# A new layout of the first two tiles' work, and nine products of the identity on PE

## The chip, the cores and the metric

The kernel runs on one core of a Trainium2 chip. The metric is device time in microseconds of one execution, taken several times; the median counts. A profile of one execution gives the trace from which the rows below come.

## What is computed

A gated cross attention and a gated feed-forward layer, in f32, on x and a context, both of 16 batches x 64 channels x 512 positions:

```
xn  = layernorm(x)                      # over the 512 positions
q   = Wq @ instance_norm(xn) + bq       # 64 x 512, for each batch
k   = Wk @ instance_norm(ctx) + bk
s   = Ws @ ctx + bs
a   = softmax(q^T k)                    # 512 x 512, for each batch
mean = a s ;  std = sqrt(relu(a s^2 - mean^2))
x   = x + tanh(g1) * (instance_norm(ctx) * std + mean)
x   = x + tanh(g2) * (layernorm(x) @ W^T)   # W from 4-bit weights, scales and zeros
```

## The kernel before, in words

Two batches are one tile of 128 partitions, so there are 8 tiles. The scores of a tile are made in 8 chunks of 128 query positions (4 for each batch b), numbered g = 0 to 63 over all tiles; chunk g belongs to tile t = g // 8. Every engine has its program written out in order, and semaphores connect them.

The query weights and key weights are multiplied first (multiply_weights, L266), so that scores are x^T (Wq^T Wk) ctx plus bias terms. To keep f32 accuracy at the speed of the rounded type fp32r, operands are split into a high part (a cast) and a low part (the rest). project(t) (L279) makes q of tile t in side_bank by three products. q is split by keep_q_hi on ACT (L434) and keep_q_lo on DVE (L609). The operands of the scores are then stacked on 128 partitions: q_both (q hi over q lo), c_both (the context's hi twice), q_with_x (q hi over x hi), c_with_bias (the context's lo over the bias rows). For b = 0 of tile 0 ACT and DVE write these stacks; for all others SP issues seven copies by DMA (stack, L211). It waits for c_lo_done before the first four and for q_lo_done before the last three. scores(g) (L287) waits for the stacks of its batch where j is 0, and does two products of 512 columns (L296, L297).

Then, chunk by chunk: DVE takes the maximum (L616), ACT the exponentials (L442), DVE the reciprocal of their sum (L623), POOL the normalised probabilities (normalise_probs, L831), PE turns them (turn, L306, four transposes), ACT copies them back (L450) and PE weighs the values with them (weigh, L322). The values come from value_product(t) (L333), kept by DVE (keep_values) and squared by POOL (square_values, L836). Scores run three chunks ahead (AHEAD_S), exponentials two (AHEAD_E), weighing two behind.

During tile t the engines also prepare tile t + 2: statistics on DVE (L559, L565), the power -0.5 on POOL (L812), xn and the context normalised on DVE (L586, L599), their hi parts cast on DVE (L594, L604), their lo parts on POOL (x_lo in split_x_lo, L818; c_lo in split_c_lo, L824), and project(t + 2) on PE at chunk 7. The weights of the feed-forward are prepared in tiles 1 to 7, and the feed-forward itself follows the last tile.

The start: SP loads x, params and the context of tile 0, then tile 1. DVE makes the statistics of x, then of the context (L539 to L550); xn, x_hi, x_lo and w_a_lo come before the context's parts. PE starts with L271 when params are there.

## Time and profile before

| | us |
|---|---|
| median of 3 runs | 186.06 |
| lowest and highest | 185.04, 186.35 |
| the profiled execution, its time | 186.42 |
| its span in the trace | 184.6 |
| PE busy in the span | 167.2 |
| DVE, ACT, POOL busy | 141.0, 118.0, 120.4 |

The span runs from the first to the last instruction of the trace; the time of the same execution is 1.8 us longer. A transfer's row stands on SPq, the queue that issues it, with the time of the issue alone; what waits for its landing names it as releaser. A column of idle time gives what ended the wait.

### The profile page before, as it was taken

The page shows a single profiled execution, that of the slowest core. Times are in us where ns is not written, and L with a number is a line of the kernel's source. Part 1 is how long each engine was busy: PE and PEld are TensorE (multiplying, and loading weights), DVE is VectorE, ACT ScalarE, POOL GpSimd, SP SyncE. Part 2 cuts the span into 40 slices and gives each one's busy share as a digit, 9 for nine tenths or more (in the row PEclk, how much of TensorE's full clock was granted, in tenths as well). Part 3 has the DMA queues.
Part 4 walks back from the last instruction along what each step waited for, and adds up shares of the span by engine and source line. Part 5 has one row for each costly group of instructions (what it writes and reads, how often), then busy time and mean ns, then how long its engine had stood idle before and what let it go on. Part 6 is the DMA issues. An engine that isn't in the chain of part 4 may idle for free.

```text
span 184.6 us, 3489 instructions
## 1 busy us (share of the span) xinstructions
PE 167.2 (91%) x1128; PEld 147.1 (80%) x1128; DVE 141.0 (76%) x311; ACT 118.0 (64%) x261; POOL 120.4 (65%) x145
## 2 busy tenths in 40 slices
PE   1554999999999999999999999999999979789992
PEld 0432889999999999999999999998789867567881
DVE  2897696689859887986988798676159679988851
ACT  2253575978598678859867885995569995232110
POOL 1455586917955896799589679944328959966310
PEclk9999999999999999999999999999999999999999
DMA  6408566883796699679679966356100000111212
GB/s 169 166 21 202 186 159 138 237 201 86 184 319 153 155 287 245 162 216 286 139 170 249 283 145 153 78 134 151 44 0 0 4 0 0 57 62 60 111 57 114
DMA packets 14321, 25.75 MB, mean 139 GB/s; under 512 B 2336, under 2 KB 2464, under 8 KB 14304
## 3 DMA queue, kind: packets, MB, share of 16 engines
q1 hardware_dynamic: 14304, 25.54, 52.2%
q8 instruction: 9, 0.15, 0.4%
q14 instruction: 8, 0.07, 0.1%
HBM read 9.67 MB, written 2.10 MB: 64 GB/s over the span
## 4 chain that ended last, share of the span: by engine, by line
PE 76%; DVE 9%; ACT 4%; issue 4%; POOL 3%; DMA 2%; SPq 0%; ACTq 0%; POOLq 0%
PE pv_bank L322 28%; PE turn_bank L306 14%; PE score_bank L296 8%; PE score_bank L297 8%; PE side_bank L333 3%; PE score_bank L377 3%; PE score_bank L371 3%; PE score_bank L370 3%; DVE X L667 2%; DMA CTX<-in_context 2%; PE side_bank L342 2%; ACT probs L442 1%; PE side_bank L283 1%; DVE result L692 1%; DVE stats L673 1%
## 5 line engine op out<-in xcount | busy, mean ns | idle before, releaser
L831 POOL TENSOR_SCALAR probs<-probs,rden 128x512 f32<-128x512 f32 x64 | 50.9, 796 | 32.2 <-DVE rden L623 32.0
L322 PE MATMUL pv_bank<-probs_t,values 128*128 128x128 f32 x512 | 67.7, 276 | 0.0
L442 ACT ACTIVATE probs<-score_bank,neg_max 128x512 f32<-128x512 f32 x64 | 44.1, 690 | 31.4 <-DVE neg_max L616 30.8
L322 PEld LDWEIGHTS pv_bank<-probs_t,values 128*128 128x128 f32 x512 | 62.4, 192 | 2.1 <-issue 1.7
L616 DVE TENSOR_REDUCE neg_max<-score_bank 128x1 f32<-128x512 f32 x64 | 43.5, 682 | 15.0 <-PE score_bank L297 14.4
L306 PE MATMUL turn_bank<-ident,probs 128*128 128x128 f32 x256 | 38.8, 275 | 1.1 <-ACT probs_t L450 1.0
L450 ACT COPY probs_t<-turn_bank 128x512 f32<-128x512 f32 x64 | 37.1, 581 | 3.2 <-PE turn_bank L306 3.0
L306 PEld LDWEIGHTS turn_bank<-ident,probs 128*128 128x128 f32 x256 | 31.1, 142 | 5.7 <-POOL probs L831 1.1
L296 PE MATMUL score_bank<-c_both,q_both 128*128 128x512 f32 x64 | 29.3, 458 | 2.3 <-ACT q_with_x L494 2.3
L297 PE MATMUL score_bank<-c_with_bias,q_with_x 128*128 128x512 f32 x64 | 26.4, 412 | 0.0
L296 PEld LDWEIGHTS score_bank<-c_both,q_both 128*128 128x128 f32 x64 | 13.0, 202 | 4.6 <-issue 2.9
L623 DVE RECIPROCAL rden<-den 128x1 f32<-128x1 f32 x64 | 9.9, 154 | 6.1 <-ACT probs L442 6.0
L297 PEld LDWEIGHTS score_bank<-c_with_bias,q_with_x 128*128 128x128 f32 x64 | 13.0, 203 | 1.7
L370 PE MATMUL score_bank<-w_hi,xt_hi 128*128 128x512 f32 x32 | 12.8, 402 | 0.0
L371 PE MATMUL score_bank<-w_lo,xt_hi 128*128 128x512 f32 x32 | 12.7, 397 | 0.0
L442 ACT ACTIVATION_READ_ACCUMULATOR probs<-score_bank,neg_max 128x1 f32 x64 | 12.6, 197 | 0.0
L634 DVE TENSOR_TENSOR VAR<-pv_bank,mean_sq 64x512 f32<-64x512 f32 x16 | 11.1, 694 | 0.5
L865 POOL TENSOR_TENSOR rstd<-var_eps,power 128x1 f32<-128x1 f32 x8 | 6.7, 834 | 7.0 <-DVE var_eps L679 7.0
L824 POOL TENSOR_TENSOR c_lo<-CTX,c_hi 128x512 fp32r<-128x512 f32 x8 | 10.7, 1337 | 0.8 <-DVE c_hi L604 0.8
L818 POOL TENSOR_TENSOR x_lo<-xn,x_hi 128x512 fp32r<-128x512 f32 x7 | 9.0, 1282 | 3.1 <-DVE x_hi L594 3.1
L860 POOL TENSOR_TENSOR CTX<-CTX,VAR 128x512 f32<-128x512 f32 x7 | 9.4, 1348 | 2.1 <-ACT VAR L465 2.1
L609 DVE SCALAR_TENSOR_TENSOR q_lo<-side_bank,b_a,q_hi 128x512 fp32r<-128x512 f32 x8 | 6.0, 749 | 5.6 <-ACT q_hi L434 5.6
(99 smaller groups left out, 243.6 us busy)
## 6 DMA issues: line engine op xcount, KB each, us to landing
c_both<-c_hi SPq DMA_DIRECT2D x30, 128.0 KB, 2.6
X<-in_x SPq DMA_DIRECT2D x8, 256.0 KB, 3.0
CTX<-in_context SPq DMA_DIRECT2D x8, 256.0 KB, 4.1
ctx_now<-in_context SPq DMA_DIRECT2D x8, 256.0 KB, 2.9
sz<-in_scales_zeros SPq DMA_DIRECT2D x4, 512.0 KB, 6.7
out<-result SPq DMA_DIRECT2D x8, 256.0 KB, 2.0
q_with_x<-x_hi SPq DMA_DIRECT2D x15, 128.0 KB, 2.3
c_with_bias<-c_lo SPq DMA_DIRECT2D x15, 128.0 KB, 2.9
```

Source lines behind the costliest of these rows:

```text
L296: pe.matmul(score_bank[g % SBANKS][:, :], q_both[b][:, rows], c_both[b][:, :], start=True, stop=False)
L297: pe.matmul(score_bank[g % SBANKS][:, :], q_with_x[b][:, rows], c_with_bias[b][:, :], start=False, stop=True).then_inc(scores_done, 1)
L306: last = pe.transpose(turn_bank[g % 2][:, P * i:P * i + P], probs[g % PROBS][:, P * i:P * i + P], ident[:, :])
L322: last = pe.matmul(pv_bank[b][:, P * j:P * j + P], values[t % 2][:, i, b, :, :].rearrange("p a c -> p (a c)"), probs_t[g % PROBS_T][:, P * ...
L370: pe.matmul(ffn_bank[u % 2][:, :], hi, w_hi[:, g, :], start=(g == 0), stop=False)
L371: pe.matmul(ffn_bank[u % 2][:, :], hi, w_lo[:, g, :], start=False, stop=False)
L442: act.activation(probs[g % PROBS][:, :], score_bank[g % SBANKS][:, :], ACT.Exp, bias=neg_max[:, c:c + 1], accum_out=den[:, c:c + 1]).then_ ...
L450: act.copy(probs_t[g % PROBS_T][:, :], turn_bank[g % 2][:, :]).then_inc(turned_kept, 1)
L616: dve.tensor_reduce(neg_max[:, c:c + 1], score_bank[g % SBANKS][:, :], AX_X, ALU.max, negate=True).then_inc(max_done, 1)
L634: dve.tensor_tensor(VAR[rows_of(b), t, :], pv_bank[b][C:P, :], mean_sq[b][C:P, :], ALU.subtract).then_inc(var_done, 1)
L824: pool.tensor_tensor(c_lo[t % 2][:, :], CTX[:, t, :], c_hi[t % 2][:, :].bitcast(F32), ALU.subtract).then_inc(c_lo_done, 1)
L831: pool.tensor_scalar(probs[g % PROBS][:, :], probs[g % PROBS][:, :], rden[:, c:c + 1], 1.0, ALU.mult, ALU.mult).then_inc(probs_done, 1)
```

## The change

It touches only the work of tiles 0, 1 and part of tile 2.

- SP loads the context of tile 0 first, then x; params go over ACT's queue. The copies of tile 0, b = 1 become four (first_stacked) in place of seven.
- PE multiplies ident by itself: spin(6) ahead of the weights' transposes, spin(1) behind them, spin(2) ahead of the first product. They write score_bank[0], which scores(0) writes anew.
- q of tile 0 is made by plain f32 products of w_a with xn (project_first), in pieces of 128 (FIRST, into turn_bank[1]) and 384 columns (REST, into side_bank). w_a_hi and w_a_lo are made later, on POOL, for project(1).
- The stacks of tile 0 are written directly from the banks, in these pieces, by ACT (hi) and DVE (lo: first_lo). The pieces of c and x for b = 1 are split between ACT, POOL and the copies.
- PE does scores 0 to 3 first, then turn(0), value_product(0); project(1) comes after turn(2), project(2) moves from chunk 7 to chunk 8.
- On DVE the maxima and reciprocals of chunks 0 to 2 stand between the statistics of tile 1 and the pieces of q. The casts x_hi and c_hi of tiles 1 and 2 move from DVE to ACT (cast_x_hi, cast_c_hi).
- On POOL, normalise_probs(0) and (1) surround the power of tile 1; after normalise_probs(2) come split_x_lo(1), square_values(0) and the memset of averages, then normalise_probs(3); split_c_lo(1) comes at chunk 2. For tile 2, the power stands behind normalise_probs(7), and split_x_lo(2) at chunk 7.

The rest of the diff renumbers semaphores. Its core:

```diff
+            sp.dma_start(CTX[:, 0, :], context_tiles[0]).then_inc(first_loaded[0][1], DMA)
             sp.dma_start(X[:, 0, :], x_tiles[0]).then_inc(first_loaded[0][0], DMA)
-            sp.dma_start(params_sb[:, :], params).then_inc(params_loaded, DMA)
-            sp.dma_start(CTX[:, 0, :], context_tiles[0]).then_inc(first_loaded[0][1], DMA)
             load(1, *first_loaded[1])
             load_ctx_now(0)
+            sp.wait_ge(first_c_both, 3)
+            sp.dma_start(c_both[1][0:C, :].bitcast(F32), c_both[1][C:P, :].bitcast(F32)).then_inc(first_stacked, DMA)
+            sp.wait_ge(first_q_hi, 4)
+            sp.dma_start(q_both[1][0:C, :].bitcast(F32), q_hi[0][C:P, :].bitcast(F32)).then_inc(first_stacked, DMA)
+            sp.dma_start(q_with_x[1][0:C, :].bitcast(F32), q_hi[0][C:P, :].bitcast(F32)).then_inc(first_stacked, DMA)
             sp.wait_ge(c_lo_done, 1)
-            stack(0, 1, *x_and_context_copies)
-            sp.wait_ge(q_lo_done, 1)
-            stack(0, 1, *q_copies)
+            sp.dma_start(c_with_bias[1][0:C, :].bitcast(F32), c_lo[0][C:P, :].bitcast(F32)).then_inc(first_stacked, DMA)
             load_ctx_now(1)
...
@@ -263,6 +293,10 @@
 
         @block.tensor
         def _(pe):
+            def spin(n):
+                for _ in range(n):
+                    pe.matmul(score_bank[0][:, FIRST], ident[:, :], ident[:, :], start=True, stop=True)
+
             def multiply_weights():
 
                 w_q, w_k = w_turned[:, 0:P], w_turned[:, P:2 * P]
@@ -270,16 +304,27 @@
                 pe.wait_ge(ident_ready, 1)
                 pe.transpose(turn_bank[0][:, 0:P], w_qk[:, 0:P], ident[:, :])
                 pe.transpose(turn_bank[0][:, P:2 * P], w_qk[:, P:2 * P], ident[:, :]).then_inc(w_turned_done, 1)
+                spin(1)
                 pe.wait_ge(w_turned_kept, 1)
-                pe.matmul(pv_bank[1][:, 0:P], w_q, w_k, start=True, stop=True)
-                pe.matmul(pv_bank[1][:, P:P + 1], w_k, b_qk[:, 0:1], start=True, stop=True)
-                pe.matmul(pv_bank[1][:, P + 1:P + 2], w_q, b_qk[:, 1:2], start=True,
-                          stop=True).then_inc(w_multiplied, 1)
+                pe.matmul(pv_bank[0][:, 0:1], w_k, b_qk[:, 0:1], start=True, stop=True)
+                pe.matmul(pv_bank[0][:, 1:2], w_q, b_qk[:, 1:2], start=True,
+                          stop=True).then_inc(biases_multiplied, 1)
+                pe.matmul(pv_bank[1][:, 0:P], w_q, w_k, start=True, stop=True).then_inc(w_multiplied, 1)
+
+            def project_first():
+
+                pe.wait_ge(xn_done, 1)
+                pe.wait_ge(w_a_ready, 1)
+                pe.matmul(turn_bank[1][:, FIRST], w_a[:, :], xn[:, FIRST], start=True, stop=True).then_inc(first_q_done, 1)
...
-                    pe.wait_ge(stacked[b], STACK * (t + 1))
+                if t > 0:
+                    if j == 0:
+                        pe.wait_ge(stacked[b], STACK * t)
+                elif g == 0:
+                    pe.wait_ge(first_c_both, 2)
+                    pe.wait_ge(first_c_lo, 1)
+                    pe.wait_ge(bias_rows_ready, 1)
+                    pe.wait_ge(first_x_rows, 1)
+                    pe.wait_ge(first_q_copied, 1)
+                    pe.wait_ge(first_q_lo, 1)
+                elif g == 1:
+                    pe.wait_ge(first_q_copied, 2)
+                    pe.wait_ge(first_q_lo, 2)
+                elif g == JC:
+                    pe.wait_ge(first_stacked, 4 * DMA)
+                    pe.wait_ge(first_q_lo, 4)
+                    pe.wait_ge(bias_rows_ready, 2)
...
 
+            pe.wait_ge(ident_ready, 1)
+            spin(6)
             multiply_weights()
-            pe.wait_ge(w_split, 1)
-            project(0)
-            pe.wait_ge(bias_rows_ready, 2)
-            for g in range(AHEAD_S):
+            spin(2)
+            project_first()
+            for g in range(AHEAD_S + 1):
                 scores(g)
-            pe.wait_ge(q_lo_done, 1)
-            project(1)
-            scores(AHEAD_S)
-            value_product(0)
-            pe.wait_ge(ident_ready, 1)
 
             for t in range(TILES):
                 for c in range(CHUNKS):
@@ -396,10 +453,17 @@
                     if c % 2 == 1 and g + AHEAD_S < LAST:
                         scores(g + AHEAD_S)
                         scores(g + AHEAD_S + 1)
-                    if c == 7 and t + 2 < TILES:
+                    if c == 7 and 1 <= t and t + 2 < TILES:
                         pe.wait_ge(s_kept, t + 2)
                         project(t + 2)
+                    if g == CHUNKS:
+                        pe.wait_ge(s_kept, 2)
+                        project(2)
                     turn(g)
+                    if g == 0:
+                        value_product(0)
+                    if g == 2:
+                        project(1)
                     if c == 3 and t + 1 < TILES:
...
@@ -477,21 +554,31 @@
                 act.copy(xt_hi[u % 2][:, :], xt_bank[u % 2][:, :]).then_inc(xt_hi_done, 1)
 
 
+            act.dma_start(params_sb[:, :], params).then_inc(params_loaded, DMA)
             act.wait_ge(w_turned_done, 1)
             act.copy(w_turned[:, :], turn_bank[0][:, 0:2 * P]).then_inc(w_turned_kept, 1)
-            act.wait_ge(params_loaded, DMA)
+            act.wait_ge(ctxn_done, 1)
+            act.copy(c_both[0][0:C, :], CTX[0:C, 0, :]).then_inc(first_c_both, 1)
+            act.wait_ge(w_multiplied, 1)
+            act.copy(w_a[:, :], pv_bank[1][:, 0:P]).then_inc(w_a_ready, 1)
+            act.copy(c_both[0][C:P, :], CTX[0:C, 0, :]).then_inc(first_c_both, 1)
+            act.wait_ge(b_ready, 1)
+            act.wait_ge(first_q_done, 1)
+            act.activation(q_both[0][0:C, FIRST], turn_bank[1][0:C, FIRST], ACT.Identity,
+                           bias=b_a[0:C, 0:1]).then_inc(first_q_hi, 1)
+            act.wait_ge(first_q_hi, 1)
+            act.copy(q_with_x[0][0:C, FIRST], q_both[0][0:C, FIRST].bitcast(F32)).then_inc(first_q_copied, 1)
+            act.copy(c_both[1][C:P, :], CTX[C:P, 0, :]).then_inc(first_c_both, 1)
+            act.wait_ge(first_q_done, 2)
+            act.activation(q_both[0][0:C, REST], side_bank[0:C, REST], ACT.Identity,
+                           bias=b_a[0:C, 0:1]).then_inc(first_q_hi, 1)
+            act.wait_ge(first_q_hi, 2)
+            act.copy(q_with_x[0][0:C, REST], q_both[0][0:C, REST].bitcast(F32)).then_inc(first_q_copied, 1)
+            act.activation(q_hi[0][C:P, FIRST], turn_bank[1][C:P, FIRST], ACT.Identity,
+                           bias=b_a[C:P, 0:1]).then_inc(first_q_hi, 1)
+            act.activation(q_hi[0][C:P, REST], side_bank[C:P, REST], ACT.Identity,
+                           bias=b_a[C:P, 0:1]).then_inc(first_q_hi, 1)
             act.activation(tanh_g[:, :], gates, ACT.Tanh).then_inc(gates_ready, 1)
-            act.wait_ge(w_multiplied, 1)
-            act.copy(w_a_hi[:, :], pv_bank[1][:, 0:P]).then_inc(w_hi_ready, 1)
-            act.wait_ge(ctxn_done, 1)
-            act.copy(c_both[0][0:C, :], CTX[0:C, 0, :]).then_inc(stacked[0], DMA)
-            act.copy(c_both[0][C:P, :], CTX[0:C, 0, :]).then_inc(stacked[0], DMA)
-            act.wait_ge(b_ready, 1)
-            act.wait_ge(q_done, 1)
-            keep_q_hi(0)
-            act.wait_ge(q_hi_done, 1)
-            act.copy(q_both[0][0:C, :], q_hi[0][0:C, :].bitcast(F32)).then_inc(stacked[0], DMA)
-            act.copy(q_with_x[0][0:C, :], q_hi[0][0:C, :].bitcast(F32)).then_inc(stacked[0], DMA)
             for g in range(AHEAD_E):
                 exponentials(g)
...
-                    if c == 0 and t + 1 < TILES:
+                    if g == 0:
+                        cast_x_hi(1)
+                    if g == 1:
+                        cast_c_hi(1)
+                    if g == 6:
+                        cast_x_hi(2)
+                    if g == 7:
+                        cast_c_hi(2)
+                    if g == 2:
+                        keep_q_hi(1)
+                    if c == 0 and 1 <= t and t + 1 < TILES:
                         keep_q_hi(t + 1)
...
                                          X[:, u, :], ALU.mult, ALU.add).then_inc(result_done, 1)
 
 
-            first_statistics()
+            def first_lo(n, b, bank, columns, hi):
+
+                dve.wait_ge(first_q_hi, n)
+                dve.scalar_tensor_tensor(q_both[b][C:P, columns], bank[rows_of(b), columns], b_a[rows_of(b), 0:1],
+                                         hi[rows_of(b), columns].bitcast(F32), ALU.add,
+                                         ALU.subtract).then_inc(first_q_lo, 1)
+
+            first_statistics(1, CTX, first_loaded[0][1], 1.0, EPS)
+            first_statistics(0, X, first_loaded[0][0], 1.0 + EPS, EPS * EPS)
+            normalise_ctx(0)
             normalise_x(0)
-            keep_x_hi(0)
-            dve.wait_ge(x_hi_done, 1)
-            dve.tensor_tensor(x_lo[:, :], xn[:, :], x_hi[0][:, :].bitcast(F32), ALU.subtract).then_inc(x_lo_done, 1)
-            dve.wait_ge(w_hi_ready, 1)
-            dve.tensor_tensor(w_a_lo[:, :], pv_bank[1][:, 0:P], w_a_hi[:, :].bitcast(F32),
-                              ALU.subtract).then_inc(w_split, 1)
-            dve.tensor_copy(b_a[:, :], pv_bank[1][:, P:P + 2]).then_inc(b_ready, 1)
-            normalise_ctx(0)
-            dve.tensor_copy(q_with_x[0][C:P, :], x_hi[0][0:C, :].bitcast(F32)).then_inc(stacked[0], DMA)
-            keep_c_hi(0)
-            dve.wait_ge(c_hi_done, 1)
-            dve.tensor_tensor(c_with_bias[0][0:C, :], CTX[0:C, 0, :], c_hi[0][0:C, :].bitcast(F32),
-                              ALU.subtract).then_inc(stacked[0], DMA)
-            dve.wait_ge(q_hi_done, 1)
-            dve.scalar_tensor_tensor(q_both[0][C:P, :], side_bank[0:C, :], b_a[0:C, 0:1],
-                                     q_hi[0][0:C, :].bitcast(F32), ALU.add, ALU.subtract).then_inc(stacked[0], DMA)
-            keep_q_lo(0)
+            dve.wait_ge(biases_multiplied, 1)
+            dve.tensor_copy(b_a[:, :], pv_bank[0][:, 0:2]).then_inc(b_ready, 1)
+            dve.wait_ge(first_c_both, 1)
+            dve.tensor_tensor(c_with_bias[0][0:C, :], CTX[0:C, 0, :], c_both[0][0:C, :].bitcast(F32),
+                              ALU.subtract).then_inc(first_c_lo, 1)
+            dve.wait_ge(xn_done, 1)
+            dve.tensor_copy(q_with_x[0][C:P, :], xn[0:C, :]).then_inc(first_x_rows, 1)
+            first_lo(1, 0, turn_bank[1], FIRST, q_both[0])
             x_statistics(1)
+            first_lo(2, 0, side_bank, REST, q_both[0])
+            maximum(0)
             ctx_statistics(1)
+            maximum(1)
+            reciprocal(0)
             finish_statistics(1)
+            maximum(2)
+            reciprocal(1)
+            first_lo(3, 1, turn_bank[1], FIRST, q_hi[0])
+            first_lo(4, 1, side_bank, REST, q_hi[0])
             normalise_x(1)
-            keep_x_hi(1)
             dve.wait_ge(gates_ready, 1)
-            for g in range(AHEAD_S):
-                maximum(g)
-                if g > 0:
-                    reciprocal(g - 1)
-            normalise_ctx(1)
-            keep_c_hi(1)
 
             for t in range(TILES):
...
@@ -732,8 +831,23 @@
                         maximum(g + AHEAD_S)
                     if g + AHEAD_E < LAST:
                         reciprocal(g + AHEAD_E)
-                    if t == 0 and c == 0:
+                    if g == 0:
                         keep_values(0)
+                        normalise_ctx(1)
+                    if g == 2:
+                        keep_q_lo(1)
+                    if g == 4:
+                        keep_values(1)
+                        x_statistics(2)
+                    if g == 5:
+                        ctx_statistics(2)
+                        finish_statistics(2)
+                    if g == 6:
+                        normalise_x(2)
+                    if g == 7:
+                        normalise_ctx(2)
+                    if t == 0:
+                        continue
                     if c == 0:
                         if t + 1 < TILES:
...
             pool.wait_ge(b_ready, 1)
-            pool.wait_ge(rstd_done, 1)
+            pool.wait_ge(first_rstd_done, 2)
             pool.tensor_copy(c_with_bias[0][C:P, :], b_a[C:P, 1:2].broadcast_to([C, N])).then_inc(bias_rows_ready, 1)
             pool.wait_ge(bias_rows_ready, 1)
             pool.tensor_copy(c_with_bias[1][C:P, :], b_a[C:P, 1:2].broadcast_to([C, N])).then_inc(bias_rows_ready, 1)
+            pool.wait_ge(xn_done, 1)
             pool.wait_ge(bias_rows_ready, 2)
-            split_c_lo(0)
+            pool.tensor_copy(q_with_x[1][C:P, :], xn[C:P, :]).then_inc(second_x_rows, 1)
+            pool.wait_ge(first_c_both, 3)
+            pool.wait_ge(second_x_rows, 1)
+            pool.tensor_tensor(c_lo[0][C:P, :], CTX[C:P, 0, :], c_both[1][C:P, :].bitcast(F32),
+                               ALU.subtract).then_inc(c_lo_done, 1)
+            pool.wait_ge(w_a_ready, 1)
+            pool.wait_ge(c_lo_done, 1)
+            pool.tensor_copy(w_a_hi[:, :], w_a[:, :]).then_inc(w_a_hi_ready, 1)
+            pool.wait_ge(w_a_hi_ready, 1)
+            pool.tensor_tensor(w_a_lo[:, :], w_a[:, :], w_a_hi[:, :].bitcast(F32), ALU.subtract).then_inc(w_split, 1)
+            normalise_probs(0)
             inverse_deviation(1)
-            pool.memset(averages[:, :], 1.0 / N).then_inc(consts_ready, 1)
-            split_x_lo(1)
-            for g in range(AHEAD_E):
-                normalise_probs(g)
-            split_c_lo(1)
+            normalise_probs(1)
 
             for t in range(TILES):
                 for c in range(CHUNKS):
                     g = CHUNKS * t + c
-                    if t == 0 and c == 0:
+                    if g == 0:
+                        normalise_probs(2)
+                        split_x_lo(1)
                         square_values(0)
+                        pool.memset(averages[:, :], 1.0 / N).then_inc(consts_ready, 1)
+                        continue
                     if c == 0 and 3 <= t < 3 + GROUPS:
...
-                    if c == 3 and t + 2 < TILES:
+                    if g == 2:
+                        split_c_lo(1)
+                    if g == 5:
+                        normalise_probs(7)
+                        inverse_deviation(2)
+                    if g == 7:
+                        split_x_lo(2)
+                    if c == 3 and 1 <= t and t + 2 < TILES:
                         inverse_deviation(t + 2)
                     if c == 4 and t > 0:
```

## Rows read from the trace of the kernel before

**Rows 1.** The page, part 4: shares of the chain that ended last, by engine.
```profile
PE 76%; DVE 9%; ACT 4%; issue 4%; POOL 3%; DMA 2%; SPq 0%; ACTq 0%; POOLq 0%
```
**Rows 2.** The chain in order of time: start us, us, engine, output and line.
```profile
1.64 3.64 DMA CTX<-in_context
...
18.42 0.43 PE side_bank L284
...
26.88 0.44 PE turn_bank L306 x4
27.32 0.89 PE side_bank L333 x8
...
43.27 0.89 PE side_bank L333 x8
```
**Rows 3.** Timeline of PE: start us, us, instruction, [idle before, releaser].
```profile
12.20 0.76 PE L296 MATMUL score_bank<-c_both,q_both 128*128 128x512 f32 x1 [2.26 <-ACT q_with_x L494]
...
17.65 0.77 PE L283 MATMUL side_bank<-x_hi,w_a_hi 128*128 128x512 f32 x1 [2.55 <-POOL x_lo L818]
...
19.92 1.91 PE L333 MATMUL pv_bank<-params_sb,ctx_now 128*128 128x128 f32 x8
...
23.34 0.58 PE L296 MATMUL score_bank<-c_both,q_both 128*128 128x512 f32 x1
...
30.19 0.48 PE L296 MATMUL score_bank<-c_both,q_both 128*128 128x512 f32 x1
30.51 0.40 PE L297 MATMUL score_bank<-c_with_bias,q_with_x 128*128 128x512 f32 x1
30.74 0.39 PE L296 MATMUL score_bank<-c_both,q_both 128*128 128x512 f32 x1
```
**Rows 4.** Windows: stretch, its length, busy us of each engine, granted clock, DMA share, GB/s.
```profile
17.60:23.50 5.90, 5.85 (x20) 5.21 (x21) 4.47 (x10) 3.48 (x8) 3.70 (x4) 1.00 0.62 187
```
**Rows 5.** Timeline of all engines, the first 7 us.
```profile
0.72 0.39 SPq L227 DMA_DIRECT2D X<-in_x  x1
...
3.53 0.69 DVE L539 BATCH_NORM_STATS2 stats<-X 128x6 f32<-128x512 f32 x1 [3.53 <-DMA X<-in_x]
...
4.08 0.48 PE L271 MATMUL turn_bank<-ident,params_sb 128*128 128x128 f32 x1 [4.08 <-DMA params_sb<-in_params]
...
4.78 0.56 POOL L880 TENSOR_TENSOR rstd<-var_eps,power 128x1 f32<-128x1 f32 x1 [3.32 <-DVE var_eps L543]
...
6.32 0.54 DVE L586 TENSOR_SCALAR xn<-X,mean_var,rstd 128x512 f32<-128x512 f32 x1
6.48 0.87 POOL L882 TENSOR_TENSOR rstd<-var_eps,power 128x1 f32<-128x1 f32 x1 [1.14 <-DVE var_eps L550]
```
**Rows 6.** Groups by line, shapes kept apart: busy us, mean ns, idle before.
```profile
L831 POOL TENSOR_SCALAR probs<-probs,rden 128x512 f32<-128x512 f32 x64 | 50.9, 796 | 32.2 <-DVE rden L623 32.0
...
L616 DVE TENSOR_REDUCE neg_max<-score_bank 128x1 f32<-128x512 f32 x64 | 43.5, 682 | 15.0 <-PE score_bank L297 14.4
...
L824 POOL TENSOR_TENSOR c_lo<-CTX,c_hi 128x512 fp32r<-128x512 f32 x8 | 10.7, 1337 | 0.8 <-DVE c_hi L604 0.8
...
L836 POOL TENSOR_TENSOR values<-values 128x512 f32<-128x512 f32 x8 | 9.1, 1140 | 1.6 <-DVE values L643 1.6
L818 POOL TENSOR_TENSOR x_lo<-xn,x_hi 128x512 fp32r<-128x512 f32 x7 | 9.0, 1282 | 3.1 <-DVE x_hi L594 3.1
```
**Rows 7.** Timeline at tile 1's copies, then q_both's transfers: issue to landing.
```profile
19.80 1.27 POOL L824 TENSOR_TENSOR c_lo<-CTX,c_hi 128x512 fp32r<-128x512 f32 x1 [0.36 <-DVE c_hi L604]
...
21.10 0.47 SPq L214 DMA_DIRECT2D q_with_x<-x_hi  x1
...
24.81 0.60 SPq L214 DMA_DIRECT2D q_both<-q_lo  x1
...
DMA to landing us min/median/max: 2.4/2.4/2.6
```
**Rows 8.** Timeline of PE in the feed-forward: its longest idle time while fast.
```profile
160.03 0.66 PE L356 MATMUL score_bank<-ident,X 128*128 128x128 f32 x4 [1.18 <-DVE X L667]
```

## What the change will do to the time, predicted from these rows

> **What bounds the kernel now.** I read the page's chain first: PE carries 76% of the chain that ended last [rows 1]. The chain in order of time then says where this holds. The value products of tiles 1 and 2 stand at 27.32 and 43.27, 15.95 us apart [rows 2]; in the PE timeline no row between them has idle time before it. So from about 23.5 to 140 us the end is set by how early PE gets into this steady sequence, and a shift there goes through to the end. Ahead of it PE waits: 2.55 us for POOL's x_lo before 17.65 [rows 2, 3].
>
> The PE timeline also shows the clock's level. A 512-column product takes 0.43 us of the chain at 18.42 (1.2 GHz) [rows 2]; at 23.34 one is shortened, and at 30.51 and 30.74 they start 0.23 us apart, the 2.4 GHz level [rows 3]. The windows' column of granted clock reads 1.00 for 17.6 to 23.5 too, so here the pace tells it [rows 4]. PE had worked without a gap for 5.9 us (17.65 to 23.5, busy 5.85 of 5.90) when it rose. Half of these 5.9 us, 2.9 us, is what the low level cost.
>
> The mark I measure from is the first scores product of tile 1 (chunk 8), at 30.19 [rows 3]. All PE work ahead of it (both projections, chunks 0 to 7, two value products, three weighings) is the same in the new kernel.
>
> **The changes, part by part.** *Loads.* The context goes first, x second, params on ACT's queue. X, params and context, issued from 0.72 to 1.64, land at 3.53, 4.08 and 5.28 [rows 2, 5]. The new context should be there between 3.5 and 4.1 (it now shares with params), I take 3.8; x between 4.4 and 5.3. The Trainium skill (Trainium Kernel Development and Optimization, Key Constraints) says that transfers from all queues run on the same 16 DMA engines, so that a second queue saves only issue time. Here two issues take the 0.92 us from 0.72 to 1.64, 0.46 each; I count no more than that for the move to ACT.
>
> *To xn.* From landing to POOL's power, statistics take 1.25 us (3.53, 4.78) [rows 5], of them 1.1 on DVE. Context 3.8 to 4.9, x to 6.0, the power 0.56 to 0.87 [rows 5] to 7.0, xn 0.56 to 7.6. Before, xn ended at 6.32 + 0.54 = 6.86 [rows 5]. This part loses 0.7 us; the full f32 product (one w_a instead of hi and lo) takes the cast, x_lo and w_a_lo out of the path behind it.
>
> *DVE after xn.* Up to reciprocal(2), DVE now has 18 instructions in one row: b_a 0.15, context lo 0.68, x rows 0.72, four pieces of q_lo (two of 128 columns at 0.34, two of 384 at 0.6, an estimate scaled down from the 0.68 of 512 columns in a maximum [rows 6]), two statistics 0.69 each, their finish 0.5, four maxima 0.68 each, three reciprocals 0.15 each, xn 0.54. The ones of a whole tensor go by L616 and L539 [rows 5, 6], those of one or two columns by an estimate of 0.15, some less than the smallest power. Sum 9.0 us; independent neighbours overlap by up to 0.08 each, which gives back 0.7 to 1.3 us. I take 8.0, so reciprocal(2) ends at 15.6 (bounds 15.2 and 16.6). PE and ACT are covered here. PE needs q rows of 128 columns to begin scores(0) at about 9.4 (12.20 before [rows 3]). ACT's casts give q's second piece at 9.7 to 10.1, when DVE reaches it. What was gained by the small first piece is 2.8 us at scores(0), and it is largely taken back in this row of DVE.
>
> *POOL after that.* Its queue from here is normalise_probs(2), split_x_lo(1), square_values(0), a memset (an estimate of 0.2, for a quarter of the columns of the 0.80), normalise_probs(3), split_c_lo(1): 0.80 + 1.28 + 1.14 + 0.2 + 0.80 + 1.34 = 5.6 us [rows 6]. Starting at 15.7 it ends at 21.3 with c_lo of tile 1. Before, that instruction ended at 19.80 + 1.27 = 21.07 [rows 7]: with all the new order, the copies of tile 1 have no earlier start.
>
> *SP.* Behind c_lo it issues four copies, then three of q; the first starts at once behind c_lo (21.07), the seventh 3.71 us behind the first (21.10, 24.81), and lands 2.4 us later [rows 7]. In the kernel before this is 24.81 + 2.4 = 27.2, and PE came only at 30.19, so the transfers were hidden with 3.0 us to spare. Now: 21.3 + 3.74 + 2.4 = 27.5.
>
> *PE to the mark.* weigh(0) waits for square_values(0), 15.7 + 0.80 + 1.28 + 1.14 = 18.9. Then at the high level: weighing 0.89, two scores 1.0 (0.32 and three times 0.23), turn 0.44, value product 0.89, weighing 0.89 (as many products), turn 0.44, weighing 0.89 = 5.4 us [rows 2, 3], at 24.4. PE stands before chunk 8 and waits 3.1 us for the copies, where it had waited for none. Queued behind that wait are turn(5) and all that follows; DVE's maximum(8) waits for it, and behind that stand reciprocal(7) and the second half of tile 2's statistics.
>
> *project(2).* It moves from before turn(7) to before turn(8), but its x_lo now stands on POOL behind probs(7), the power, square_values(1) and probs(8). Counted from the mark: maximum(8) ends at 1.3, reciprocal(7) 1.4, statistics 2.6, power 3.4, square 4.5, probs(8) 5.3, x_lo 6.6. PE is there at 5.9 (four scores 2.0, three turns 1.3, three weighings 2.7, the overlap at their seams included). Loss 0.7 us. c_lo of tile 2 then ends near 7.9 after the mark, its copies land by 14.1, and chunk 16 is due at 16; hidden.
>
> *The nine products of ident.* Each is an f32 product of 128 columns, as one of the four in the value product at the low level: 1.91 us for four with the last drain, 0.43 each [rows 3]. Six from 1.5 to 4.1 end as params lands; one lies beside ACT's copy of w_turned; two (0.86) end at 7.1, ahead of xn at 7.6. They cost nothing; if xn came at 6.9 the last would cost 0.2.
>
> *Their use.* PE is then at work from 1.5 to about 8.7 with gaps of at most 0.5 us, longer than the 5.9 us after which the clock rose before. So I expect the high level from about 7.5 on. But what it brings up to the mark is small. The second piece of the first product (384 columns, four passes) takes 0.65 instead of 1.3 us, and DVE and ACT feel 0.4 us of that. The rest falls into PE's wait.
>
> **The sum.** The mark moves from 30.19 to 27.5, minus 2.7; project(2) gives 0.7 back: minus 2.0 us. The profiled span of 184.6 us becomes 182.6. That execution took 186.42 us, and the median of the runs is 186.06, so 184.0 us from the median. Bounds: reciprocal(2) from 15.2 to 16.6, landing 2.4 to 2.6 [rows 7], POOL's six instructions within 0.3 us, project(2)'s wait 0 to 1.0: 182.9 to 185.4.
>
> **Rivals.** *(a) The clock falls in the wait.* PE idles 3.1 us before the mark. While the level was high, the trace before has no idle stretch over 1.18 us [rows 8], and that did not lower it, so 3.1 us is untried. If it falls, PE restarts low and pays as it did before: 5.9 us at half pace, 2.9 us. The end is 186.9 us, slower than before. It decides against the kernel from a low stretch of 4.0 us on, twice the gain of 2.0. For it: the work between 8.7 and 18.9 is thin too. Against it: 3.1 us is short, and PE was busy for 5.4 us ahead of it. The Trainium skill (TensorE: Matmul & The Clock Gate, the part on the HAM clock gate) holds the low level for the default to which idleness brings the engine back; no row here shows a fall, and by that rule alone this rival would be the time.
>
> *(b) The copies don't hold PE.* If POOL were done with c_lo near 18 (fewer waits of its queue), PE would pass the mark at 24.4: minus 5.8 + 0.7, 180.9 us. Against it stands the sum of its queue.
>
> *(c) The products of ident raise no clock in time.* The rise then comes in the stretch from about 15.3 on, near 21 by the 5.9 us seen before. PE's work to the mark would end near 26, still before the copies, which come 0.4 us later: 184.4 us. The spins then do nothing and the change still gains.
>
> *(d) The start is longer.* Context lands at 4.1, x at 5.3, DVE's instructions overlap nowhere and POOL's run at their longest: the mark at 28.7, 185.2 us, no change that can be told.
>
> **How the numbers follow.** The forecast 0.45, (a) 0.20, (b) 0.08, (c) 0.12, (d) 0.15. The likeliest gives 184.0, own range 182.9 to 185.4. The range for 8 in 10 takes in (c), (d) and most of (a), and leaves out (b) and a fall that lasts longer: 182.3 to 187.0. About 1% is what a measurement of this kernel can tell from no change, so the bounds are 184.2 and 187.9. Faster: two thirds of the forecast 0.30, (b) 0.08, a third of (c) and some of (d) 0.10, together 0.48. Slower: the worse part of (a) and what I have not seen, 0.12. Within 1%: 0.40.
>
> **What would show it.** Right: L296 of chunk 8 near 27.5, with 3 us of idle PE before it that end with a copy's landing; c_lo of tile 1 ending near 21.3; project(2) waiting for x_lo; 512-column products 0.23 us apart at 10 us. (a) shows as products 0.43 us apart after 27.5; (b) as PE without idle time before chunk 8; (c) as the pace of 0.43 at 15 us; (d) as chunk 8 past 28.5. The forecast is wrong if the steady sequence from tile 2 on takes more than its 16 us a tile.

## The result, and the profile after

The changed kernel takes 189.03 us (median; the kernel before beside it 186.35), a ratio of 1.0147 with a 95% interval of 1.0087 to 1.0206. Two further takings gave 1.0136 (1.0098 to 1.0175) and 1.0129 (1.0090 to 1.0168). It is slower by 1.3 to 1.5%; forecast was 184.0, faster by 1.1%.

The first profiled execution took 339.56 us, with every product at the pace of the low clock level (1.2 GHz) or a little slower from first to last; it stands apart from all others (187.8 to 189.9) and is left out of the comparison. The trace read here is of the second taking of the same kernel (e1, below): time 188.34 us, span 186.5 us, against 184.6 before.

The timeline of PE around the mark (chunk 8) and at the value product of tile 2, of the changed kernel:

```profile
24.71 1.06 PE L381 MATMUL pv_bank<-probs_t,values 128*128 128x128 f32 x8
29.05 0.50 PE L357 MATMUL score_bank<-c_both,q_both 128*128 128x512 f32 x1 [3.28 <-DMA q_both<-q_lo]
...
35.94 0.47 PE L328 MATMUL side_bank<-x_hi,w_a_hi 128*128 128x512 f32 x1 [0.78 <-POOL x_lo L933]
...
42.61 1.13 PE L381 MATMUL pv_bank<-probs_t,values 128*128 128x128 f32 x8 [1.00 <-DVE VAR L732]
...
44.94 1.06 PE L394 MATMUL side_bank<-params_sb,ctx_now 128*128 128x128 f32 x8
```

The mark is at 29.05, where it was at 30.19 [rows 3]: 1.14 us gained. The wait before it is there, it ends with the landing of q_lo's copy, and it is new. But the value product of tile 2 starts at 44.94. Before, its row in the timeline is at 43.10 (the chain counts it from 43.27 [rows 2]). From mark to value product it was 12.91 us and is 15.89. That is 2.98 us lost behind the mark, 1.84 us in sum, and the span is 1.9 us longer. From there to the end both kernels take the same time (141.6 and 141.5 us).

The chain in order of time shows what sets each of the two pieces (start us, us, what):

```profile
16.93 0.69 POOL probs L948
17.62 1.40 POOL x_lo L933
19.02 1.00 POOL values L953
20.02 0.14 POOL averages L1028
20.16 0.67 POOL probs L948
20.83 1.26 POOL c_lo L941
...
26.64 2.37 DMA q_both<-q_lo
...
31.79 0.73 POOL rstd L926
32.52 0.02 issue
32.54 1.27 DVE xn L682
...
39.10 0.60 ACT q_hi L501
39.70 0.02 issue
39.73 0.75 DVE q_lo L707
40.48 0.60 DVE stats L650
41.08 0.59 DVE neg_max L714
...
41.77 0.70 DVE VAR L732
```

The upper part is the POOL queue and the copies, in the order of the forecast. The lower part is what the forecast did not follow to its end: behind the mark, the chain leaves PE and runs through POOL, DVE and ACT for 13 us.

### The profile page after: what moved, and what is told of

The parts are those of the page before. It is cut to its first block, busy times and chain, and to the rows that moved or that the text cites. A ratio compares the mean times of both kernels' runs of the same rounds, so it can differ in the third digit from the quotient of the medians.

```text
span 337.8 us, 3532 instructions
## 1 busy us (share of the span) xinstructions
PE 332.5 (98%) x1147; PEld 268.2 (79%) x1147; DVE 138.4 (41%) x305; ACT 127.4 (38%) x269; POOL 121.2 (36%) x148
## 4 chain that ended last, share of the span: by engine, by line
PE 98%; ACT 1%; DVE 0%; issue 0%; POOL 0%; POOLq 0%; ACTq 0%
PE pv_bank L381 36%; PE turn_bank L367 18%; PE score_bank L357 9%; PE score_bank L358 9%; PE score_bank L438 4%; PE score_bank L431 4%; PE score_bank L432 4%; PE side_bank L394 4%; PE side_bank L403 2%; PE score_bank L298 1%; PE score_bank L417 1%; PE side_bank L417 1%; PE side_bank L329 1%; PE side_bank L330 1%; PE side_bank L328 1%; PE pv_bank L394 1%
## 5 line engine op out<-in xcount | busy, mean ns | idle before, releaser
L381 PE MATMUL pv_bank<-probs_t,values 128*128 128x128 f32 x512 | 133.2, 445 | 0.0
L381 PEld LDWEIGHTS pv_bank<-probs_t,values 128*128 128x128 f32 x512 | 126.5, 331 | 6.8 <-issue 2.9
L367 PE MATMUL turn_bank<-ident,probs 128*128 128x128 f32 x256 | 72.5, 439 | 0.0
L367 PEld LDWEIGHTS turn_bank<-ident,probs 128*128 128x128 f32 x256 | 46.5, 188 | 23.3 <-issue 12.3
L357 PE MATMUL score_bank<-c_both,q_both 128*128 128x512 f32 x64 | 48.2, 753 | 0.5 <-DVE q_both L797 0.5
L358 PE MATMUL score_bank<-c_with_bias,q_with_x 128*128 128x512 f32 x64 | 43.5, 680 | 0.0
L438 PE MATMUL score_bank<-w_hi,xt_lo 128*128 128x512 f32 x32 | 17.4, 695 | 0.0
L394 PE MATMUL side_bank<-params_sb,ctx_now 128*128 128x128 f32 x56 | 14.6, 446 | 0.0
L394 PEld LDWEIGHTS side_bank<-params_sb,ctx_now 128*128 128x128 f32 x56 | 13.8, 330 | 0.3
L431 PEld LDWEIGHTS score_bank<-w_hi,xt_hi 128*128 128x128 f32 x32 | 9.9, 308 | 4.9 <-issue 4.4
```

Of the source, the lines that this page charges most:

```text
L357: pe.matmul(score_bank[g % SBANKS][:, :], q_both[b][:, rows], c_both[b][:, :], start=True, stop=False)
L358: pe.matmul(score_bank[g % SBANKS][:, :], q_with_x[b][:, rows], c_with_bias[b][:, :], start=False, stop=True).then_inc(scores_done, 1)
L367: last = pe.transpose(turn_bank[g % 2][:, P * i:P * i + P], probs[g % PROBS][:, P * i:P * i + P], ident[:, :])
L381: last = pe.matmul(pv_bank[b][:, P * j:P * j + P], values[t % 2][:, i, b, :, :].rearrange("p a c -> p (a c)"), probs_t[g % PROBS_T][:, P * ...
L394: last = pe.matmul(values_bank(t)[:, P * i:P * i + P], ctx_now[t % 2][:, P * i:P * i + P], w_s, start=True, stop=True)
L431: pe.matmul(ffn_bank[u % 2][:, :], hi, w_hi[:, g, :], start=(g == 0), stop=False)
```

## The experiments

In the table "context" is the landing of tile 0's context where it is loaded first, "mark" the start of chunk 8, "VP" the start of tile 2's value product, in the trace of each kernel; times are medians, the ratio is to the kernel before beside it.

| kernel | context | mark | VP | between | time | ratio (95%) |
|---|---|---|---|---|---|---|
| before |  | 30.19 | 43.10 | 12.91 | 186.06 | |
| e1 changed, again | 4.41 | 29.05 | 44.94 | 15.89 | 188.29 | 1.0136 (1.0098, 1.0175) |
| e2 layout only | 4.31 | 29.17 | 45.24 | 16.07 | 188.12 | 1.0111 (1.0078, 1.0144) |
| e3 ident products only |  | 30.43 | 43.34 | 12.91 | 186.39 | 1.0017 (0.9998, 1.0036) |
| e4 tile 2 early | 4.24 | 29.75 | 44.28 | 14.53 | 187.56 | 1.0075 (1.0047, 1.0102) |
| e5 c_lo early | 4.00 | 27.42 | 43.32 | 15.90 | 187.00 | 1.0037 (1.0009, 1.0065) |
| e6 both | 4.02 | 27.78 | 41.72 | 13.94 | 183.72 | 0.9889 (0.9849, 0.9930) |
| e7 wait filled | 3.90 | 28.40 | 44.30 | 15.90 | 187.96 | 1.0104 (1.0073, 1.0135) |
| e8 tile 2 early, filled | 3.99 | 29.14 | 42.08 | 12.94 | 185.80 | 0.9988 (0.9970, 1.0005) |
| e9 both, no ident products | 3.98 | 28.51 | 41.77 | 13.26 | 185.10 | 0.9945 (0.9914, 0.9975) |
| e10 both, filled | 4.93 | 28.39 | 41.46 | 13.07 | 183.86 | 0.9893 (0.9864, 0.9922) |
| e11 casts on DVE | 4.04 | 28.39 | 42.94 | 14.55 | 186.56 | 1.0022 (0.9996, 1.0047) |
| e12 changed, third | 3.89 | 28.93 | 45.79 | 16.86 | 188.54 | 1.0129 (1.0090, 1.0168) |

One trace is one execution. The landing of the context differs by 1 us between the earliest and the latest of them (3.89, 4.93) and moves DVE's row, the mark and VP with it; e1, e12, e7 and e11 run the same program up to the wait before the mark, and their marks are 29.05, 28.93, 28.40 and 28.39. The column "between" is free of this. The traced executions of e6 (185.18 us) and e10 (184.86) are 1.5 and 1.0 us slower than the medians beside them.

**e1, e2, e3: which part costs.** e2 leaves out the nine products, e3 is the kernel before with them alone.

In the changed kernel, for e2:

```diff
-                spin(1)
...
-            spin(6)
...
-            spin(2)
```

> The changed kernel as it is, taken again for a trace and more times, since the first trace shows TensorE at the 1.2 GHz pace from the first to the last product (337.8 us). Theory A (the wait before chunk 8 lets the clock fall): chunk 8 starts near 27.5, products before it run 0.23 us apart, behind it for some us 0.43 apart, and the whole takes 188 to 190 us. Theory B (the clock never rises early, the products of ident bring nothing): products 0.43 us apart until past 20 us, chunk 8 later than 28. If the level of the first trace is a second outcome that comes with this program, one or more of the runs will be near 338 us again.

> The new layout without the nine products of ident. Theory A: TensorE is low until its continuous stretch and then waits before chunk 8 just as long or a little less; the clock can fall here too: 186 to 190 us. Theory B or any theory in which the ident products do the harm: about 184 to 185 us, no run near 338 us. My forecast had 184.4 for a start in which they raise no clock.

> The kernel before with the nine products of ident alone (six ahead of the transposes, one behind, two ahead of the first projection). If they raise the clock early and it holds: 2 us less than before, about 184. If they bring no clock: as before, within 0.5 us. If the products of ident are what sends a run to the low level for good: a run near 338 us, or a median slower than before by 1 to 3 us.

The loss is the layout's: without any product of ident it is still 188.12, and these products alone change nothing that can be told. They do raise the clock early where the new layout keeps PE at work: in e1 the 512-column products are 0.23 us apart from 11.94 on (0.43 until past 14 in e2). In the trace of the kernel before with them (e3) PE idles 2.26 and 2.56 us on the way, the products at 13.43 and 18.88 are 0.43 us apart, and the rise comes at 23.6 as ever. That is one execution, with a mean granted clock of 0.998; 8 of e3's 12 have 0.960 to 0.972, which records a fall and so an earlier rise, and they take no less time (185.89 to 186.89, the other four 185.96 to 186.71). The mark hardly moves with the nine products between e1 and e2 (29.05, 29.17): rival (c)'s point. But in e1 the rise came late. In the traces of e7 and e11 it comes at about 5 us, the row of DVE from xn to reciprocal(2) is 0.3 us shorter (8.6 for 8.9), and the mark is at 28.4, with a context that landed 0.4 to 0.5 us earlier.

In e2's trace the clock falls behind the wait. The windows (stretch, length, busy of PE, PEld, DVE, ACT, POOL, granted clock, DMA share, GB/s), e2:

```profile
30.00:31.00 1.00, 1.00 (x7) 0.91 (x6) 1.00 (x3) 0.34 (x1) 0.21 (x1) 0.73 0.91 209
31.00:32.00 1.00, 1.00 (x6) 1.00 (x6) 0.93 (x6) 0.92 (x3) 0.58 (x2) 0.50 0.85 199
...
34.00:35.00 1.00, 1.00 (x9) 0.91 (x9) 0.00 (x0) 1.00 (x2) 0.83 (x2) 1.00 0.95 361
```

So rival (a) happens in that execution, and in e1's it doesn't, and both end alike. Two theories remained: A, the fall is the loss; C, the loss is in the other engines' rows behind the mark.

**e4, e5, e6, e7: the two pieces apart.** e4 moves all of tile 2's preparation ahead of what waits for the mark; e5 moves c_lo of tile 1 up in POOL's queue; e6 is both; e7 fills PE's wait with 14 products of ident.

e5, on POOL:

```diff
                         split_x_lo(1)
+                        split_c_lo(1)
                         square_values(0)
...
-                    if g == 2:
-                        split_c_lo(1)
```

e4, on DVE, then on POOL (where the power also moves behind normalise_probs(6)); both casts on ACT move to g == 5 and project(2) on PE back to chunk 7:

```diff
+                    if g == 5:
+                        reciprocal(7)
+                        normalise_x(2)
+                        normalise_ctx(2)
                     if g + AHEAD_S < LAST:
                         maximum(g + AHEAD_S)
...
                         normalise_probs(7)
+                        split_x_lo(2)
+                        split_c_lo(2)
```

e7, on PE, ahead of the wait for the copies of chunk 8:

```diff
+                if g == CHUNKS:
+                    pe.wait_ge(exp_done, g - SBANKS + 1)
+                    for _ in range(14):
+                        pe.matmul(score_bank[g % SBANKS][:, FIRST], ident[:, :], ident[:, :], start=True, stop=True)
```

> The changed kernel, with all of tile 2's preparation (second statistics, power, xn, both casts, both lo parts) put ahead of what waits for chunk 8, and project(2) back at chunk 7. The copies of tile 1 keep their time. Theory C (the time is lost behind the wait: 3.0 us between chunk 8 and the value product of tile 2, because every engine's row of tile 2 hangs on chunk 8): chunk 8 stays near 29.05, the value product comes 12.9 to 13.1 us behind it as before the change, and the whole goes to 185.0 us, 3 us less than the changed kernel. Theory A (clock falling in the wait is the price): stays at 187 to 188.

> The changed kernel, with split_c_lo(1) on POOL moved ahead of square_values(0), the memset and normalise_probs(3). Its end moves from 22.08 to about 20.3, so if the copies set chunk 8, that comes at 27.2 in place of 29.05, PE's wait shrinks from 3.3 us to under 1, and the whole is 1.8 us less: 186.3 to 186.5. If the copies did not set it, no change: 188.2.

> Both edits together. By theory C with the copies as the start: 1.8 + 3.0 us less than the changed kernel, 183.4 us, 2.7 us less than the kernel before. By A alone: about 185 to 186.

> The changed kernel, with fourteen further products of ident by itself in PE's wait ahead of chunk 8 (3.1 us at the high level), so that PE is not idle there. Theory A (the clock falls in that wait and this is the loss): about 186 us and no products 0.43 us apart behind 29 us. Theory C: within 0.4 us of the changed kernel, since PE waits for DVE and POOL afterwards anyway.

e5: the copies set the mark. From the start of probs(2) to c_lo's end POOL takes 3.34 us in place of 5.15, 1.8 us less, and the mark moves up by 1.63, of which 0.41 is the earlier landing of the context in that execution. The 15.9 us behind it stay as they are, and 1.3 us of the time come back (1.8 expected).

e6 falls by 4.6 us from e1, by more than the two edits gain alone (0.7 and 1.3), and is 1.1% faster than the kernel before. e7 removes the fall of the clock in five of its six executions (mean clock 0.999 or 1.000; the changed kernel has that in 2 of 16) and gains 0.3 us at most; between mark and value product stand 15.90 us, as in e1, whose trace has no fall. With the layout as it was changed, A is not the loss.

e4 missed its number by 2.6 us, and its trace says why. PE after the mark of e4, timeline and windows:

```profile
29.75 0.50 PE L357 MATMUL score_bank<-c_both,q_both 128*128 128x512 f32 x1 [4.14 <-DMA q_both<-q_lo]
30.09 0.47 PE L358 MATMUL score_bank<-c_with_bias,q_with_x 128*128 128x512 f32 x1
30.35 0.63 PE L357 MATMUL score_bank<-c_both,q_both 128*128 128x512 f32 x1
30.77 0.63 PE L358 MATMUL score_bank<-c_with_bias,q_with_x 128*128 128x512 f32 x1
```

```profile
25.60:29.70 4.10, 0.01 (x1) 0.00 (x0) 1.66 (x5) 1.14 (x2) 2.76 (x4) 1.00 0.82 187
...
30.40:33.70 3.30, 3.30 (x15) 3.00 (x14) 1.54 (x3) 2.04 (x5) 2.14 (x3) 0.50 0.89 202
33.70:37.00 3.30, 3.30 (x24) 2.95 (x23) 1.28 (x3) 2.21 (x4) 0.42 (x1) 1.00 0.74 245
```

Behind the mark PE has no idle row in e4, so the knock-on is gone; but PE, idle for 4.14 us, now pays for the low level: 3.3 us at 0.50, half of them lost, 1.6 us. 12.91 + 1.6 = 14.5, which is what stands in the table. The mark itself came 0.7 us later, since the copies land later: SP's two issues of c_both take 2.71 us there (1.25 in e1), that of c_with_bias 0.60 (1.41), the last one of q_both 0.81 (0.60).

**e8, e9, e10: the clock, once PE alone sets the time.**

e8 is e4 with 18 products of ident ahead of chunk 8, in the manner of e7; e9 is e6 without the nine products. e10 is e6 with, behind project(1):

```diff
+                        pe.wait_ge(exp_done, 4)
+                        spin(6)
```

> Tile 2's preparation early (as before) and eighteen products of ident (4.0 us at the high level) in PE's wait ahead of chunk 8. With nothing but PE left behind the wait, the clock's fall is on the path: in the trace without the filling, 3.4 us of products at the low pace behind the mark, 1.6 us lost. If the idle wait lowers the clock, this kernel keeps the pace of 0.23 us, the value product of tile 2 comes 12.9 us behind the mark, and the time is 186.0 us. If the clock falls for another reason, 187.5 as without it.

> The kernel with both repairs (183.7 us), without any product of ident. If these bring something once nothing else holds PE: slower by up to 1 us. If DVE's and POOL's rows set the mark, as the traces with and without them say (29.05 and 29.17): the same within 0.5 us.

> The kernel with both repairs, and six further products of ident (1.3 us) in the wait of 1.36 us ahead of the first weighing, behind which its trace shows 3.4 us at the low pace and 1.5 us lost. If the idle times lower the clock: 183.4 us in all runs and none near 185.3. If not, no difference: 183.7 with some at 185.

e8 is the test of both theories at once. Filling the wait brought e7 at most 0.3 us, and brings e8 1.76 us over e4 (187.56, 185.80): 12.94 us between mark and value product, the number of the kernel before. (Its mark, 29.14, is where the 18 products end, not where the copies land.) The fall of the clock is real and costs 1.6 us where PE sets the time; in the changed kernel as it stood, PE waited for others later anyway, and most of the fall was hidden in these waits. e12's trace has the longest: low from 27.3, 2.0 us into an idle time of 3.66 us, to 34.1, and 16.86 between, 1.0 more than in e1.

The mean granted clock of each execution gives a price for the changed kernel as it stood. A mean of 0.991 over 186 us is a low stretch of 2 x 0.009 x 186 = 3.3 us. Its 16 executions (without the one of 339.56 us), over the three takings:

| mean clock | low stretch, worked out | executions | time |
|---|---|---|---|
| 1.000 | none | 2 | 187.84, 188.34 |
| 0.989 to 0.991 | 3.3 to 4.1 us | 9 | 187.98 to 188.69 |
| 0.982, 0.973 | 6.7, 10.0 | 3 | 189.24, 189.66, 189.03 |
| 0.964 | 13.4 | 2 | 189.83, 189.92 |

Some 3 to 4 us at the low level cost 0 to 0.5 us there, and 6.7 us or more, in one stretch (as in e12's trace, 189.24 us) or in several, cost 1 to 2; the mean does not say where a stretch lies. Even without any fall the changed kernel stays 1.4 and 2.2 us behind the median of the kernel before beside it (187.84 to 186.39, 188.34 to 186.11).

e9 is 1.4 us slower than e6 (185.10 beside 186.17, 183.72 beside 186.3): outside both of the numbers expected, "within 0.5 us" and "up to 1 us". Without the nine, PE is at the low level until about 17. In e9's trace c_lo of tile 1 then waits 1.02 us for ACT's c_hi and ends at 20.88, in e6's at 19.88 (the context landed at 3.98 and 4.02), and the mark comes at 28.51 in place of 27.78. e10 shows no difference to e6 in the median (183.86, 183.72), though its trace keeps the high level where e6's falls to 0.50 from 21.0 to 23.7; the two traces can't be compared at the mark, since in e10's the context landed 0.91 us later; its mark waits 0.87 us for the copies. The clock fell in that execution too, earlier: the granted clock is 0.50 from about 8.4 to 11.7.

**e11, e12: where behind the mark.** e11 puts the two casts of tile 2 back on DVE, behind normalise_x(2) and normalise_ctx(2), with the guards and the count of casts (ACT_CASTS) that go with them, nothing else.

```diff
-    ACT_CASTS = 2
+    ACT_CASTS = 1
...
-                    if g == 6:
-                        cast_x_hi(2)
-                    if g == 7:
-                        cast_c_hi(2)
...
+                        keep_x_hi(2)
...
+                        keep_c_hi(2)
```

> The changed kernel, with the two casts of tile 2 (x_hi, c_hi) back on DVE, at the same chunks as they had on ACT; all else stays. In the trace of the changed kernel ACT idles 2.03 us before the cast of x_hi with exponentials(9) queued behind it. If this queueing on ACT makes most of the 3.0 us lost behind the mark: the value product of tile 2 comes 14 us behind the mark in place of 15.9, and the whole is 1 to 2 us less, 186.5. If the late statistics and project(2) at chunk 8 make it, whichever engine casts: 188.3 as before.

> The changed kernel once more, for the time near 338 us that one of its first five executions took with every product at the low level. If that is a frequent outcome of this program, it shows again in these; if it is a rare one, all are 188 to 190 us.

e11 is 186.56, as expected. The rows of the changed kernel that it undoes (e1, timeline of ACT and DVE):

```profile
32.54 1.25 DVE L682 TENSOR_SCALAR xn<-X,mean_var,rstd 128x512 f32<-128x512 f32 x1 [0.17 <-POOL rstd L926]
...
33.83 0.62 ACT L506 CAST x_hi<-xn 128x512 fp32r<-128x512 f32 x1 [2.03 <-DVE xn L682]
34.36 0.68 ACT L519 ACTIVATE probs<-score_bank,neg_max 128x512 f32<-128x512 f32 x1
...
37.85 0.70 ACT L519 ACTIVATE probs<-score_bank,neg_max 128x512 f32<-128x512 f32 x1
...
38.99 0.70 ACT L501 ACTIVATE q_hi<-side_bank,b_a 128x512 fp32r<-128x512 f32 x1
```

ACT stands 2.03 us before the cast, and exponentials(9), whose maximum ended at 32.30, is queued behind it until 34.36. From the mark, exponentials(9) and (10) start at 5.3 and 8.8 us, q_hi of tile 2 at 9.9. In e11 they start at 3.3, 6.7 and 8.5 (its timeline of ACT and a window of PE):

```profile
31.67 0.69 ACT L519 ACTIVATE probs<-score_bank,neg_max 128x512 f32<-128x512 f32 x1 [0.25 <-DVE neg_max L711]
...
35.09 0.69 ACT L519 ACTIVATE probs<-score_bank,neg_max 128x512 f32<-128x512 f32 x1 [0.41 <-DVE neg_max L711]
...
36.86 0.69 ACT L501 ACTIVATE q_hi<-side_bank,b_a 128x512 fp32r<-128x512 f32 x1 [0.51 <-PE side_bank L330]
```

```profile
28.39:42.94 14.55, 14.55 (x95) 13.31 (x96) 12.11 (x31) 10.22 (x23) 8.90 (x11) 0.88 0.68 171
```

VAR ends 11.9 us behind the mark in place of 13.4. PE is busy in all of the 14.55 us to the value product, where it idled 2.0 us in e1's 15.89, and what is left over 12.91 is a low stretch of 3.4 us (0.50 from 29.0 to 32.4), as in e4. So with the casts back no wait of PE is left in this execution: 1.3 us of the 3.0 are gone, and the other 1.6 have the size of the fall. Not all of that would come back without a fall: x_lo of tile 2 ends at 35.35 in e11, 7.0 us behind the mark, and PE would be at project(2) 5.9 us behind it (an estimate, 35.88 less the mark and the 1.6), so that it would wait there again. e11's executions without a fall (186.24, 186.32) are hardly faster than its fastest with one (186.32). By the medians the casts cost 1.7 us (to e1) to 2.0 us (to e12, taken beside it).

## Why the prediction was wrong

- *PE sets the end, and a shift at the mark goes through.* Half right. A shift goes through, but only while nothing else holds PE between mark and steady sequence. I left the work behind the mark as it was before (12.91 us of PE), plus 0.7.
- *To xn.* 7.6 forecast, 7.97 in e1's trace, since the context landed at 4.41 for 3.8 (3.89 and 7.44 in e12's). The method holds; the landing varies.
- *DVE's row.* This is the first term mis-sized. reciprocal(2) ends at 16.83, not 15.6, and the row from xn takes 8.9 us for 8.0. DVE stood 0.5 us for ACT's q pieces (0.50 idle before L797 at 10.88 in e1's DVE timeline), and its neighbours overlapped less than I took.
- *POOL's queue.* 16.93 to 22.08 is 5.15 us for 5.6. Right; e5 confirms that it sets the copies.
- *SP.* From c_lo to the last landing 6.9 us for 6.1: one issue took 1.41 us in place of 0.60. Mark 29.05 for 27.5. So the first error is 1.5 us, and the mark was still earlier than before, as forecast.
- *The wait of 3.1 us before the mark.* 3.28 measured, and it is what the changed kernel shows as its longest new wait. Right. e7, which fills it and gains 0.3 us at most, shows that it is not PE's idleness there that lost the time.
- *project(2).* 0.7 forecast, 0.78 measured. Right in place and size, and behind it is the step that failed: the sum has this 0.7 as the only loss behind the mark and puts every other wait there at nothing. I stopped at turn(8). I named reciprocal(7) and the statistics as queued behind DVE's wait, and followed only POOL from there. I did not follow ACT, whose casts of tile 2 (which the change had just put there) wait for xn with exponentials(9) and (10) behind them; and those hold the turn of keep_q_hi(2), keep_q_lo(2) and, behind them on DVE, the variance that weigh(8) needs. What lies between mark and value product is 2.2 us more than the 0.78; e11, with the casts alone put back, has none of the idle time left.
- *Rival (a).* Its mechanism happens in some executions (e2, e12, and e4). Its price was 2.9 us by the stretch of the kernel before; it is 1.6 us in e4, and 0 to 0.5 us in most executions of the changed kernel, by the table of mean clocks. So it was not the reason for 189. The Trainium skill's sentence (TensorE: Matmul & The Clock Gate, the part on the HAM clock gate), that idleness brings the low level back, agrees with the traces of e2, e4, e11 and e12, whose granted clock falls to 0.50 in or behind waits of 3.2 to 4.1 us; in e1's it stayed at 1.00 behind 3.28 us.
- *Rival (c).* It said the nine products do nothing up to the mark. Right for e1 and e2 (29.05, 29.17); where the rise comes at 5 us (e7, e11) DVE's row is 0.3 us shorter, near the 0.4 us of the forecast, and in the repaired kernel the nine are worth 1.4 us (e9).
- The range (182.3 to 187.0) left out that two waits could come in a row behind the mark. The two errors, 1.5 and 2.3 us, add to 3.8, and -2.0 + 3.8 = +1.8, the 1.9 us of the spans. Within the first, xn is 0.4 us late, DVE's row 0.9, SP 0.8, and POOL gives 0.5 back. The medians differ by 2.1 to 2.7 us, some 0.3 to 0.8 more than this pair of spans; the executions with 6.7 us and more at the low level fit that part.

## What to carry to other kernels

When a change makes an engine stall, follow the stall through every engine's queue until nobody waits any more; the wait you find on the busiest engine is only the first. An engine that is given a helper's work in program order gives its own urgent work the helper's lateness: two casts moved from DVE to ACT cost 1.7 to 2.0 us here (e11), with the same work in all. And put preparation for a later tile ahead of what waits for a transfer, not behind it: with that and one instruction moved up in POOL's queue, the same layout is 1.1% faster than the kernel before (e6), where it was 1.4% slower.

## What the runs showed of the hardware

- The granted clock fell to 0.50 behind idle times of TensorE of 3.20 us (e2), 3.29 (e11) and 4.14 (e4), each time 0.5 to 1.3 us after the work had begun again, and within one of 3.66 us (e12). It did not fall in e1 behind 3.28 us. It came back after 2.7 to 5.1 us of work at the low level. In e10 it fell within an idle time of 1.13 us, at about 8.4, and in e6 within one of only 1.36 us that followed a thin stretch (2.58 us of work in 3.6):

```profile
16.00:19.60 3.60, 2.58 (x14) 1.59 (x12) 2.93 (x8) 3.30 (x8) 3.06 (x3) 1.00 0.41 143
19.60:21.00 1.40, 0.07 (x1) 0.00 (x1) 0.57 (x1) 1.29 (x4) 1.40 (x3) 0.84 0.00 0
21.00:23.70 2.70, 2.67 (x10) 2.53 (x11) 0.18 (x1) 0.54 (x2) 1.37 (x3) 0.50 0.89 204
```

- The first rise varies between executions: with the nine products, and PE at work from 1.51 us on with few gaps, it comes at about 5 us in the traces of e7, e10 and e11 and at 9 to 11 us in those of e1, e4, e5, e6, e8 and e12.
- The column reads 1.00 at the low pace as long as the clock has not yet risen in an execution ([rows 4]); it shows falls, not the low level at the start. The execution of 339.56 us is the extreme: PE busy 332.5 of 337.8 us, four products with f32 operands 1.89 us apart in place of 0.89 (1.71 at the low level in e12), and a mean clock of 1.00. TensorE never rose in it although it was hardly idle. It was one of 17 executions of this kernel, and none of the 76 of the kernels that carry the nine products in other settings (e3, e4, e5, e6, e7, e8, e10, e11) showed it; what brought it about stays open.
- DVE's tensor_scalar on xn took 1.25 us beside POOL's square of the values (e1 at 32.54, e11 at 31.88), and 0.55 where POOL was idle for most of it (e1 at 15.49). That is 0.7 us of the chain behind the mark, whichever engine casts.
